# Moving the second norm's turn behind the last attend, and its router into the next body

## The reference

```
h   = layernorm(x)
att = softmax((h Wq + bq)(ctx Wk + bk)^T / 4) (ctx Wv + bv)     # 16 heads of 16
x   = x + tanh(g_xattn) * (att Wo + bo)
n2  = layernorm(x)                                              # the second norm
logits = n2 Wr + br                                             # the router, 8 experts
gate   = softmax over the 2 largest logits
x   = x + tanh(g_ffn) * sum over the 2 experts of gate * (relu(n2 W1 + b1) W2 + b2)
```

## Time and profile before

| | |
|---|---|
| median of 3 runs | 963.71 us (963.53 to 966.58) |
| the profiled execution's own time | 961.2 us |
| its span in the profile | 959.4 us |
| PE busy | 814.8 us, 85% of the span |
| PEld busy | 552.9 us, 58% |
| DVE busy | 584.8 us, 61% |
| ACT busy | 419.7 us, 44% |
| POOL busy | 378.4 us, 39% |
| chain that ended last | PE 70%, DVE 8%, issue 7%, POOL 5% |
| PE waiting for POOL's xn2b at the transposes, whole run | 18.7 us, 11 times |

### The profile page before, as it was taken

How to read it: one execution, slowest core, us unless ns; L and a number is a source line. 1 busy time by engine, 2 the same in 40 slices (tenths; PEclk the granted TensorE clock), 3 DMA queues, 4 the chain that set the end, 5 groups by cost and what they waited for, 6 DMA issues and landing times.

```text
span 959.4 us, 21544 instructions
## 1 busy us (share of the span) xinstructions
PE 814.8 (85%) x6484; PEld 552.9 (58%) x6485; DVE 584.8 (61%) x1015; ACT 419.7 (44%) x777; POOL 378.4 (39%) x399
## 2 busy tenths in 40 slices
PE   4589999999999998751569999999999999999920
PEld 3346555555555555431257777777777777777710
DVE  3466777767676767435945555555555555555547
ACT  2066777767676766631033333333333333333300
POOL 4113333444343441230033555555555554555210
PEclk9699999999999999955569999999999999999975
DMA  3344556555555542238011111111111111112069
GB/s 119 105 128 156 178 154 183 178 168 158 172 159 171 158 152 90 78 126 279 0 44 40 47 48 45 49 55 49 44 49 47 52 49 44 49 46 53 29 217 330
DMA packets 93936, 103.07 MB, mean 107 GB/s; under 512 B 9478, under 2 KB 80588, under 8 KB 93772
## 3 DMA queue, kind: packets, MB, share of 16 engines
q1 hardware_dynamic: 81900, 77.95, 26.3%
q0 software_dynamic: 7488, 20.46, 7.0%
q10 hardware_dynamic: 4512, 4.20, 1.3%
HBM read 67.03 MB, written 35.39 MB: 107 GB/s over the span
## 4 chain that ended last, share of the span: by engine, by line
PE 70%; DVE 8%; issue 7%; POOL 5%; ACT 3%; DMA 3%; SPq 3%; DVEq 0%; POOLq 0%; ACTq 0%
PE banks L1411 20%; PE banks L1397 7%; PE banks L1398 7%; PE banks L1399 7%; PE banks L1182 7%; PE banks L1256 5%; POOL xn2b L551 3%; PE banks L1244 3%; PE banks L1223 2%; PE banks L1296 2%; PE banks L1384 2%; PE banks L1267 2%; PE banks L1163 2%; PE banks L1211 1%; DVE hot_col L1059 1%
## 5 line engine op out<-in xcount | busy, mean ns | idle before, releaser
L1411 PE MATMUL banks<-wall,hh 128*128 x624 | 222.7, 379 | 0.5 <-DVE yb L1111 0.5
L807 ACT ACTIVATE hid<-banks,b_col 128x256 f32<-128x256 f32 x312 | 131.0, 471 | 209.0 <-PE banks L1399 113.5
L906 DVE TENSOR_REDUCE negmax<-banks 128x4 f32<-128x1024 f32 x128 | 155.5, 1215 | 38.8 <-PE banks L1223 38.7
L1398 PE MATMUL banks<-xl,wall 128*128 128x256 f16 x624 | 171.0, 274 | 0.0
L1397 PE MATMUL banks<-xh,wall 128*128 128x256 f16 x624 | 171.0, 274 | 0.0
L1399 PE MATMUL banks<-xh,wall 128*128 128x256 f16 x624 | 171.0, 274 | 0.0
L618 POOL DMA_INDIRECT y_rows<-yb,dest_idx x78 | 106.7, 1367 | 162.4 <-DVE yb L1111 138.3
L732 ACT ACTIVATE probs<-banks 128x1024 f32<-128x1024 f32 x128 | 131.1, 1024 | 63.0 <-PE banks L1244 61.8
L1411 PE MATMUL banks<-wall,hl 128*128 x624 | 157.3, 273 | 0.0
L1109 DVE SCALAR_TENSOR_TENSOR yb<-banks,b_b 128x256 f32<-128x256 f32 x78 | 33.1, 425 | 133.0 <-PE banks L1411 133.0
L1103 DVE TENSOR_TENSOR hl<-hid,hh 128x1024 f16<-128x1024 f32 x78 | 95.6, 1225 | 2.7
(11 more groups left out here) (160 smaller groups left out, 1198.1 us busy)
## 6 DMA issues: line engine op xcount, KB each, us to landing
wst<-in_L_ffn_W SPq DMA_DIRECT2D x32, 512.0 KB, 3.9
k_parts<-kparts SPq DMA_DIRECT2D x48, 128.0 KB, 2.2
ks<-k_parts SPq DMA_DIRECT2D x64, 96.0 KB, 2.3
q_parts<-qparts SPq DMA_DIRECT2D x48, 128.0 KB, 2.0
qs<-q_parts SPq DMA_DIRECT2D x64, 96.0 KB, 2.3
xin<-in_x SPq DMA_DIRECT2D x16, 256.0 KB, 4.8
cin<-in_ctx SPq DMA_DIRECT2D x16, 256.0 KB, 5.3
xres<-in_x SPq DMA_DIRECT2D x16, 256.0 KB, 3.1
```

The source lines that it names most:

```text
L807: ins = nc.scalar.activation(hid[half][:, c % (HC // 2), :], banks[:, b, c % 2 * TS:(c % 2 + 1) * TS], ACT.Relu, bias=b1_col[:, ds(e * HC ...
L906: nc.vector.tensor_reduce(negmax[:, c, 8 * (g // 2):8 * (g // 2) + 8].rearrange("p (m g p2) -> p m g p2", m=2, g=2)[:, :, g % 2, :], banks ...
L1398: nc.tensor.matmul(dst, hi, xl[par][:, m, :], start=False, stop=False)
L1411: ins = nc.tensor.matmul(dst, h_[:, c, s * P:(s + 1) * P], w_, start=(c == 0 and k == 0), stop=(c == HC - 1 and k == 1))
```

## The change

On PE, norm2_T moves from in front of attend of step 7 to behind it. The router leaves the end of body m, where it took batch m-2, and stands in step 0 of body m+1 behind k (as router(m-3)), before attend of step 0; router(15) follows all bodies. Its wait for nm_evac goes, the one for ctxT_evac stays. On DVE the logits move from behind the reduce of step 7 to behind the reduce of step 0 of the next body, before k_low; those of batch 15 follow all bodies. The streams of ACT, POOL and SP are as they were. No instruction is added or taken away, and none changes its shape.

```diff
             splits = within(m, 3, 2 * W_KEPT + 2)
-            return maxima, ahead, turns, attention, post, weights, splits
+            judged = within(m, 3, NB + 1)
+            return maxima, ahead, turns, attention, post, weights, splits, judged
...
 # DVE
                     if maxima:
                         reduce(m, w)
+                    if judged and w == 0:
+                        router(m - 3)
...
-                    elif w == 7 and post:
-                        router(m - 2)
...
+            router(NB - 1)
             for i in range(6, len(LATE)):
                 late_low(i)
...
 # PE
-            def router(n, turns, maxima):
+            def router(n):
                 pe.wait_ge(x2T_evac, n + 1)
-                if turns:
+                if within(n, 0, NB - 5):
                     pe.wait_ge(ctxT_evac, n + 5)
-                elif maxima:
-                    pe.wait_ge(nm_evac, 2 * n + 5)
...
                         if ahead:
                             k(m + 1, 1 - par, 0)
                             k(m + 1, 1 - par, 1)
+                        if judged:
+                            router(m - 3)
...
-                    elif u == 7:
-                        if post:
-                            norm2_T(m - 2)
                     if attention:
                         attend(m - 1, 1 - par, u)
                     if u == 7 and post:
-                        router(m - 2, turns, maxima)
+                        norm2_T(m - 2)
 
             bodies(pe, body)
+            router(NB - 1)
```

## The result

The changed kernel takes 954.58 us (median of 4 runs, 952.02 to 958.72) beside 963.62 us for the kernel before on the same chip. The ratio of the runs is 0.989, with a 95% interval of 0.9856 to 0.9925. That is 9.0 us less; 956.2 was forecast, in a range of 952.0 to 964.0. The four times form two pairs, 952.0 and 952.7, 956.5 and 958.7, and the median stands between them. Repeated later on another chip, it took 952.76 us (7 runs, 952.06 to 961.38) beside 965.31: 0.9907 (0.9865 to 0.9948). Both kernels scatter over some 9 us, and their times follow the mean clock of the run: 961.8 us at 0.920 and 970.5 at 0.908 before, 952.0 at 0.928 and 961.4 at 0.916 after.

The account below looks back on a forecast made before the run. PE was taken as the busiest engine, its joints waiting for exp and POOL's xn2b. Terms -4.0 + 1.2 + 0.6 + 1.1 - 6.4 = -7.5 us gave 953.7 profiled, 956.2 as median; range 952.0 to 964.0.

Parts of the forecast that it names:

- ten late joints at unchanged clock: Passages between bodies at joints 4 to 13: each gains 0.4 us, PE and DVE 0.2 each; -4.0 us in all.
- four slow spells gone: Spells at 1.2 GHz at joints 7, 9, 11 and 13 vanish, 1.6 us each; -6.4 us.
- the two early joints: Behind bodies 2 and 3: transposes lose the gap where they were free, 0.6 us each; +1.2 us.
- bodies 15 and 16: Joints 14 and 15: ACT copies x2T later, directly ahead of its next exp, 0.3 us each; +0.6 us.
- end of stage one: Logits behind late_low(2) delay turn_out of body 17; late_low(5) brings back 1.0 us; net +1.1 us.
- the new wait at turn_max: At a late joint, turn_max waits 0.22 us for the x2T copy, a wait the router had hidden.
- k_low came 1.0 us sooner: On DVE at a late joint, k_low was to start 0.9 us sooner, closing PE's 0.30 us wait for the reduce.
- the six joints that kept their clock: Late joints with clock 1.00 before: said to show the same idle time with less of the router next to it.
- The third rival: Two waits with thin work between bring spells at every late joint, ten instead of four: +8.5 us, 972.2; chance 0.10.
- turn_out of body 17: At the end of stage one, it starts 2.1 us later because the logits stand behind late_low(2).
- slow spells at other joints: Sign against the prediction: these in the profile after, or a wait for DVE in step 1, would make it wrong.

Follow-up runs that it names:

- g_router_before_k: Against b_router_next: on PE the router stands in front of k in step 0, right behind turn_max; 950.65 us.
- a_turn_behind: Against the kernel before: transposes of xn2b moved behind attend of step 7, router at once behind them, still at the end of the body; 992.0 us.
- f_turn_behind_wide: Against a_turn_behind: the router's matmuls stream 128 columns of Wo instead of 8 of Wr; 972.84 us.
- b_router_next: Against the changed kernel: transposes of xn2b back in front of attend of step 7; router and logits stay in the next body; 946.84 us.
- d_old_end: Against the changed kernel: in body 16 transposes again before attend, router(14) behind it, its logits before late_low(2); 953.31 us.
- b_again: The same kernel as b_router_next, timed once more beside the changed kernel on the same chip; 947.35 us.
- j_wide_after: Against the changed kernel: the router's matmuls stream 128 columns of Wo instead of 8 of Wr; 951.92 us.
- h_after_again: The changed kernel as it is, run again for more times and a second trace; 952.76 us.
- c_wide_before: Against the kernel before, order untouched: the router's eight matmuls stream 128 columns of Wo instead of 8 of Wr; 956.61 us.
- e_router_next_end: Against b_router_next: router(14) stays at the end of body 16 on both engines, ahead of late_low(2); 946.60 us.
- i_logits_behind_k_low: Against b_router_next: DVE adds the logits' bias behind k_low instead of in front of it; 950.08 us.

## Why the prediction came out right

The forecast was 7.5 us, and 9.0 us came (first comparison). The terms, between the profiled executions before (961.2 us) and after (956.5):

| step | predicted | measured |
|---|---|---|
| ten late joints at unchanged clock | -4.0 | -5.0 |
| four slow spells gone | -6.4 | -6.4 |
| the two early joints | +1.2 | +1.0 |
| bodies 15 and 16 | +0.6 | 0.1 without the spell, +3.8 with it |
| end of stage one | +1.1 | +0.7 |
| all before body 3 and behind stage one | 0 | +1.0 |

The measured column comes from the ends of the exponentials of step 7. From body 4 to body 14 it is 373.81 - 136.04 = 237.77 us before and 364.21 - 137.86 = 226.35 after, 11.4 less. Four spells of 1.6 are 6.4 of it and 5.0 are left. From body 2 to body 4 it is 44.29 before and 45.29 after. The column sums to -4.9 us with the spell, as the spans do; the run without it (952.06) is 9.1 us faster than the profiled one before.

**How much of it was luck.** The mechanism held in its two main terms. That the total came so near is in part chance. The profiled run before (961.2 us, clock 0.920) was faster than all four timed beside the first comparison (963.5 to 966.6), and the forecast carried the 2.5 us between it and the median over unchanged; the late joints gained 1.0 more than forecast; and the late spell, which the forecast lacked, adds 3.7 in some runs. These errors partly cancel in a median that falls between two groups of runs.

**The late joint.** Its path on PE was right to 0.13 us, the new wait at turn_max included (0.23, worked out 0.22). The gain per joint is 0.5 instead of 0.4, and k_low came 1.0 us sooner instead of 0.9. g_router_before_k shows that half of it comes from k going first: with the router in front of k, 0.27 of the 0.5 are lost.

**The clock.** Here the prediction had said that PE's idle time is the same at all ten joints, that the spells stand at the end of the router, and that taking the router away should end them. The wide router shows that its columns matter: same order, same waits, same busy time, no spell. One reading in the prediction was wrong, though. It said that the six joints that kept their clock have less of the router next to the idle time, and that what differs at the four is exactly what the change separates. In the profile before, the router begins 1.61 to 1.66 us behind the last exp at all ten (1.61 or 1.62 at the four), in the same order, so the rows do not tell the four from the six. The full 6.4 us came, but why four joints and not ten stays open. The Trainium skill ("TensorE: Matmul & The Clock Gate", section "What's actually happening") says that the gate follows how busy PE has recently been. Read as idle time alone, that rule does not hold in this kernel: 5.76 us of busy time go with 0.79, 5.75 with 1.00. The third rival, spells at every joint, did not happen. What it described, two waits with thin work between, stands in a_turn_behind, which lost 28 us, and in f_turn_behind_wide, which kept a spell with 128 columns. In both, the waits are 0.90 and 0.69 us; in the changed kernel they are 0.90 and 0.23, and no joint of the loop has a spell.

**Early joints and end.** Both lost about what was worked out, from the order of transposes and attend and of late_low(2) and the logits: turn_out of body 17 comes 5.5 us behind the last exp instead of 3.7, 1.8 later where 2.1 was worked out. b_router_next gives the early joints back, and d_old_end the end, in its trace if not in its median. The term for bodies 15 and 16 looks right without the spell (0.1 for 0.6), but only because two effects cancel: with the router moved alone (b_router_next) these two bodies are 2.5 us shorter than before (2.0 in b_again), and the transposes behind attend cost that again. The prediction had only ACT's copy in this term.

**What the prediction did not have.** A spell ahead of joint 15 appears in one of the two profiles of the changed kernel, where bodies 15 and 16 take 3.7 us more than in the other. The forecast took the best row for the clock in the loop and had no term for the bodies behind it. It had named slow spells at other joints as a sign against itself, and this is one, though the time stayed in the range. The profiles tie this spell to the transposes behind attend: with them there, five of six have a spell at joint 14 or 15 (changed, a_turn_behind, d_old_end, f_turn_behind_wide, j_wide_after; not h_after_again), and with them in front none of seven (before, c_wide_before, b_router_next, b_again, e_router_next_end, g_router_before_k, i_logits_behind_k_low). Why, and why it comes only in some runs, was not settled. Bodies 15 and 16 have less work for PE, and from attend of step 7 to the next one body 16 takes 19.4 us here without the spell and 18.4 in b_router_next, but no run took these apart.

It also treated the change as one. Of its two halves, one does all the good and the other, on top of it, costs 5 to 8 us.

## What to carry to other kernels

Where two chains reach an engine together, swapping which of them it serves first gained nothing here; what gained was taking the piece that depends on the result (here the router, which depends on the copy of the transposed rows) out of the joint and putting dense work between. When a long instruction stream alternates between the two clock levels, look at what the matmuls just ahead of each fall pass through the array, not only at the idle time: eight matmuls with 8 columns close behind a wait of 1.1 us went with spells that cost 6.4 us in the profiled run, and with 128 columns the spells were gone. Compare the mean clock of the runs before their times. Split a change that moves two things into its halves, because here the better kernel was one of them.

## What the runs showed that was not expected

A kernel that streams sixteen times as many columns in its router, and so computes other logits, is faster by 7.7 us, with the same instructions in number and a router 0.1 us longer. The order with the transposes behind attend and the router directly behind them pays more than once for its bubbles: three of the six spells in the loop last 6.8 us, twice as long as those in the loop of the kernel before, and its time rose by 28 us for joints that are only 0.34 us longer each at full clock.
